# Retention layer: the product of scores and decay mask in two instructions, and a weighted sum that waits for each of them

## The reference

```
decay = log(1 - 2**(-5 - arange(H)))
mask = where(diff >= 0, exp(decay * diff), 0);  mask = mask / sqrt(mask.sum(-1))
qr = q * cos + rotate(q) * sin;   kr = k * cos + rotate(k) * sin
qk = einsum('bhsd,bhtd->bhst', qr, kr) * mask
qk = qk / clip(abs(qk.sum(-1)), 1)
out = einsum('bhst,bhtd->bhsd', qk, vr)
out = (out - mean) / sqrt(var + 1e-5);  out = silu(g) * out;  return out @ Wo + bo
```

## Time and profile before

| what | value |
|---|---|
| median of three runs | 3287.5 us (3285.61 to 3289.51) |
| span of the profiled execution, first to last instruction | 3276.3 us |
| PE busy | 2592.6 us, 79% of the span |
| DVE busy | 1690.3 us, 52% |
| ACT busy | 997.8 us, 30% |
| TensorE clock granted, mean | 0.915 of full |

### The profile page before, as it was taken

The page is one execution under the profiler, slowest core; times in us unless marked ns, Lnnn a source line. Parts: engine busy times, 40 slices in busy tenths (PEclk is TensorE's granted clock), DMA queues, the critical chain, the costliest instruction groups (busy, mean ns, idle before and its releaser), DMA issues.

```text
span 3276.3 us, 52997 instructions
## 1 busy us (share of the span) xinstructions
PE 2592.6 (79%) x23038; PEld 1853.6 (57%) x23038; DVE 1690.3 (52%) x4079; ACT 997.8 (30%) x1389; POOL 355.3 (11%) x605
## 2 busy tenths in 40 slices
PE   4666468888899887896778789777897778977778
PEld 2444156777777676664556455554555555555554
DVE  5666725656665654603376532665326654167540
ACT  3444312222232222031223432324323243232432
POOL 0111000111001100073010001100011000010000
PEclk8888559999999998898899999989999899998999
DMA  2000000000000000236400000000000000000000
GB/s 83 1 1 3 0 1 2 8 8 8 2 8 8 8 8 11 86 45 115 119 1 1 1 7 1 1 1 1 7 1 1 1 1 7 1 1 1 1 1 26
DMA packets 39354, 48.14 MB, mean 15 GB/s; under 512 B 7169, under 2 KB 36369, under 8 KB 38354
## 3 DMA queue, kind: packets, MB, share of 16 engines
q1 hardware_dynamic: 33490, 40.43, 4.2%
q0 software_dynamic: 5632, 4.33, 1.1%
HBM read 31.82 MB, written 12.91 MB: 14 GB/s over the span
## 4 chain that ended last, share of the span: by engine, by line
PE 56%; DVE 28%; ACT 7%; issue 4%; POOL 3%; DMA 1%; SPq 0%; DVEq 0%; POOLq 0%; ACTq 0%
PE banks L2397 7%; PE banks L871 6%; DVE wide_area L2273 4%; PE banks L2598 4%; DVE wide_area L1751 3%; PE banks L2386 2%; PE banks L1371 2%; PE banks L2171 2%; PE banks L1336 2%; PE banks L1170 2%; DVE xs L900 1%; PE banks L1404 1%; DVE weights L2090 1%; PE banks L1678 1%; PE banks L2180 1%
## 5 line engine op out<-in xcount | busy, mean ns | idle before, releaser
L2598 PE MATMUL banks<-wA 128*128 128x128 f32 x2664 | 362.8, 289 | 4.2 <-ACT xf L932 2.1
L2598 PEld LDWEIGHTS banks<-wA 128*128 128x128 f32 x2664 | 335.8, 202 | 23.2 <-issue 15.9
L892 DVE BATCH_NORM_STATS2 stats<-banks 128x6 f32<-128x128 f32 x208 | 46.4, 286 | 368.0 <-PE banks L871 340.4
L2273 DVE TENSOR_REDUCE wide_area<-banks 128x8 f32<-128x2048 f32 x64 | 146.8, 2293 | 106.8 <-PE banks L2171 106.8
L907 POOL TENSOR_TENSOR rstd<-moments,eps 128x4 f32<-128x4 f32 x56 | 11.2, 199 | 1454.9 <-DVE moments L896 1454.9
L2254 ACT ACTIVATE weights<-banks 128x2048 f32<-128x2048 f32 x64 | 120.1, 1877 | 99.5 <-PE banks L2180 99.5
L1751 DVE TENSOR_REDUCE wide_area<-banks 128x16 f32<-128x1024 f32 x80 | 94.1, 1218 | 43.9 <-PE banks L1664 43.5
L1717 ACT ACTIVATE weights<-banks 128x2048 f32<-128x2048 f32 x32 | 59.6, 1876 | 95.8 <-PE banks L1678 95.8
L2397 PE MATMUL banks<-wide_area,big 128*128 128x512 f32 x192 | 85.7, 592 | 0.0
L2090 DVE TENSOR_TENSOR weights<-banks,wC 128x2048 f32<-128x2048 f32 x32 | 72.2, 2287 | 24.1 <-PE banks L1977 24.1
L907 POOL TENSOR_TENSOR smalls<-smalls,eps 128x4 f32<-128x4 f32 x16 | 3.2, 199 | 726.2 <-DVE smalls L896 726.2
(11 more groups left out here) (765 smaller groups left out, 6077.1 us busy)
## 6 DMA issues: line engine op xcount, KB each, us to landing
big<-in_wE SPq DMA_DIRECT2D x1, 4096.0 KB, 13.9
weights<-long_kernel SPq DMA_DIRECT2D x8, 512.0 KB, 7.5
conv<-wide_area SPq DMA_DIRECT2D x16, 256.0 KB, 2.5
wC<-in_wC SPq DMA_DIRECT2D x1, 3012.0 KB, 17.3
wC<-in_wG SPq DMA_DIRECT2D x1, 2971.0 KB, 20.1
big<-in_wT SPq DMA_DIRECT2D x1, 2560.0 KB, 11.4
x_all<-in_xT SPq DMA_DIRECT2D x1, 2048.0 KB, 10.5
total<-spread SPq DMA_DIRECT2D x8, 256.0 KB, 2.3
```

What stands on the lines that cost most here:

```text
L892: dve.bn_stats(m.stats[:, i, :], self.tokens(i)).then_inc(*sg.up("dve", f"stats{i}"))
L2273: return dve.tensor_reduce(m.peaks[:, k % 2, :, :].rearrange("p t (r c) -> p r t c", r=4)[:, :, :, SPARE[j]], m.bank[:, :, :].rearrange("p ...
L2598: pe.matmul(bank[:, 0:P], m.ident, m.ident, start=True, stop=True)
```

## The change

The product becomes two instructions of 128 x 1024: `upper{i}` covers banks 0 and 1 (heads 0 to 7), `masked{i}` banks 2 and 3. Both follow the one wait for the scores. On PE the state group and the weighted sum are split in the same way: wait for `upper`, state matmuls and eight weighted sums of banks 0 and 1, then wait for `masked`, state matmuls and eight weighted sums of banks 2 and 3. The number of matmuls is the same. ACT still waits for the last of them.

```diff
-            dve += f" masked{i}{before} neg{i} denom{i} eps{i} sum{i} centre{i}{after}"
+            dve += f" upper{i} masked{i}{before} neg{i} denom{i} eps{i} sum{i} centre{i}{after}"
...
-            pe.wait_ge(*sg.done("dve", f"masked{i}", n))
-            if i % 2:
-                for r in range(4):
-                    rows = slice(32 * r, 32 * r + 32)
-                    pe.matmul(bank[:, r, 0:P], m.state[rows, i // 2, :], m.qf[rows, i * P:(i + 1) * P], start=True, stop=False)
-            for r in range(4):
-                for j in range(4):
-                    v = (i * H + 4 * r + j) * (HV + 1)
-                    mm = pe.matmul(bank[32 * j:32 * j + 32, r, 0:P], m.retflat[:, v:v + 32],
-                                   m.weights[:, (4 * r + j) * P:(4 * r + j + 1) * P], start=(i % 2 == 0), stop=True)
+            for step, half in (("upper", (0, 1)), ("masked", (2, 3))):
+                pe.wait_ge(*sg.done("dve", f"{step}{i}", n))
+                if i % 2:
+                    for r in half:
+                        rows = slice(32 * r, 32 * r + 32)
+                        pe.matmul(bank[:, r, 0:P], m.state[rows, i // 2, :], m.qf[rows, i * P:(i + 1) * P], start=True, stop=False)
+                for r in half:
+                    for j in range(4):
+                        v = (i * H + 4 * r + j) * (HV + 1)
+                        mm = pe.matmul(bank[32 * j:32 * j + 32, r, 0:P], m.retflat[:, v:v + 32],
+                                       m.weights[:, (4 * r + j) * P:(4 * r + j + 1) * P], start=(i % 2 == 0), stop=True)
...
-            dve.tensor_tensor(m.weights.rearrange("p (h q) -> p h q", h=H),
-                              bank[:, :, :].rearrange("p r (j q) -> p (r j) q", j=4),
-                              m.causal[:, 0:P].unsqueeze(1).broadcast_to([P, H, P]), ALU.mult).then_inc(*sg.up("dve", f"masked{i}"))
+            for step, half in (("upper", 0), ("masked", 1)):
+                dve.tensor_tensor(m.weights[:, half * 1024:half * 1024 + 1024].rearrange("p (h q) -> p h q", h=H // 2),
+                                  bank[:, 2 * half:2 * half + 2, :].rearrange("p r (j q) -> p (r j) q", j=4),
+                                  m.causal[:, 0:P].unsqueeze(1).broadcast_to([P, H // 2, P]), ALU.mult).then_inc(*sg.up("dve", f"{step}{i}"))
```

## The result

Beside the kernel before on the same chip the changed kernel took 3267.64 us (median of 6 runs, 3258.01 to 3273.84) against 3286.93 (6 runs, 3282.02 to 3290.99). The ratio of this comparison is 0.9925, 95% interval 0.9901 to 0.9949. It is not the quotient of these two medians, which is 0.9941 (19.3 us). The forecast, 3274.5 of 3287.5, is 0.9960. So the direction and the mechanism held. By its ratio the first comparison came out 12 us lower than forecast (0.9925 x 3287.5 = 3262.8, under the range's low end of 3267), by its medians 6 us lower (3268.2). The stage itself, read from the traces, gained 16 to 18 us where 13.0 were forecast.

A forecast was written before the change was run, and what follows sets the result against it. It took PE standing still for each pair's whole first product, much of it at 1.2 GHz, as the bound. Terms summed to 13.0 us: 3276.3 less 13.0 is 3263.3, plus 11.2 around the span 3274.5; range 3267 to 3289.

The forecast's parts named there:

- the mechanism: In the tile pairs, PE starts sums on the first half product; shorter gaps bring back the full clock: 13.0 us.
- the range's low end: Whole kernel: 3267 us, a little under 3268.7, the case with all of C's scores and free state groups (4.0 us more).
- A: First tile pair of an iteration: full clock before its second sum, gain 1.16 us in three iterations, 0.36 in one; 3.8.
- D: Last tile of lane 1, standing alone: no wait removed, second state group costs 0.43 us in each of four iterations; -1.7.
- B: Second tile pair of an iteration: PE's gap shortened and full clock kept, gain 1.06 us four times; 4.2.
- C: Third tile pair of an iteration: full clock back at about 1725.7, gain 1.3 us four times; 5.2.
- Rival 1: In the stage's tile pairs, the clock stays as it was and gains and losses cancel: 3287.5 us, chance 0.29.
- rival 2: Odd tiles: second state group and way back cost another 0.74 us (0.43 at full clock); 10.6 us slower, 3298, chance 0.11.
- The 12 waits of the earlier trace: PE's state groups waiting for the product: 11.5 us, read as one wait of some 1 us per pair, three pairs, four iterations.
- first tile: First tile of lane 0: its last half product comes later, uncovered, costing 0.08 us each, 0.3 us in all.
- C's scores: First scores of the third pair: 2.09 us to 1.17 at the full clock, counted in two iterations of four; 1.8.
- free state groups: Second state groups costing nothing: 0.43 us more in each A and D, some 0.15 in C; part of the 3268.7 case.

The follow-up runs named there:

- experiment 10: Kernel before, products whole, with scores of each pair's second tile repeated and 3, 5, 8 and 8 filler matmuls before later scores: 3259.04 us, ratio 0.9913.
- third trace: The changed kernel, unedited, compared a third time with the kernel before: 3271.83 us against 3285.68, ratio 0.9964.
- again: The changed kernel, unedited, timed and profiled a second time beside the kernel before: 3273.54 us against 3291.39, ratio 0.996.
- Experiment 9: The change in the three tile pairs only, plus 3, 5, 8 and 8 filler matmuls before scores (half an earlier run's count): 3261.6 us, ratio 0.9927.
- products only: The change with its product in two instructions, but PE waiting for both, sums and state groups whole: 3290.9 us, ratio 0.9977 to the kernel before.
- experiment 2: Kernel before, product whole, with scores of each pair's second tile computed over again while PE waits: 3271.56 us, ratio 0.9948.
- pairs only: The change without its split in lane 0's first and lane 1's last tile; second run, beside half the fillers: 3262.43 us, ratio 0.9931 to the kernel before.

## Why the prediction was right, and where it was not

**Right: the mechanism.** Split at the same full clock, the pairs gain 0.32, 0.31 and 0.30 us (A 5.99 to 5.67, B 5.55 to 5.24, C 5.55 to 5.25). That is 0.9 an iteration (44.31 to 43.33 from experiment 10 to 9; both have the same fillers, and the scores that 10 repeats fall into PE's waits), less 0.53 for D (0.45 on PE, the rest ahead of its state group): 0.4, some 1.6 us in the whole kernel. At the half clock C gained 0.2 (6.66 to 6.47) where nothing was forecast. So the sum for a clock that stays was near, and the rest of the 16 to 18 us is the clock, as forecast. Rival 1 fell with A and B off its intervals in all twelve iterations of the change's three traces, and with C off in ten. So did rival 2: the second state group costs what the forecast took, 0.43 forecast and 0.42 to 0.45 measured. The Trainium skill, TensorEngine Tiling (Array Packing), Key Properties, says that a switch of the tiling mode drains TensorE; no run here shows a state group without its switch, so that price isn't seen by itself and lies within the 0.45.

**Right: the pairs' own intervals.** A 5.63 forecast (1698.88 to 1704.51), 5.67 measured; B 5.20 (1709.59 to 1714.79), 5.24 measured. In the forecast it is DVE's last half that lets PE finish A, and the traces bear this out. A takes 5.67 us with its first 3 us at the half clock (the change, iteration 2) and at the full one (third trace, iteration 1):

```profile
2119.50:2122.50 3.00, 3.00 (x36) 1.13 (x32) 2.98 (x3) 0.00 (x0) 0.00 (x0) 0.50 0.02 5
```

```profile
1705.70:1708.70 3.00, 2.03 (x40) 0.77 (x35) 2.95 (x3) 0.00 (x0) 0.00 (x0) 1.00 0.00 0
```

**Misread, without moving the sum.** The 12 waits of the earlier trace rows are not one for each pair: they are the first waits of B and C and the second one of A, whose first stands on line 1988. That a pair's first wait is about 1 us comes out all the same. And the clock's fall at 1712.1 had more than a single gap before it:

```profile
1707.81 1.14 PE L1977 MATMUL banks<-spread,gates 32*128 32x512 f32 x8 [0.68 <-DVE segvals L2107]
```

**Mis-sized: what the clock gives around C and D.** The forecast's terms beside the gains that the three traces of the change show, in us over four iterations:

| stretch | forecast | change | again | third |
|---|---|---|---|---|
| first tile to A | -0.3 | -1.3 | -1.2 | 0.2 |
| A to B (term A) | 3.8 | 4.1 | 4.1 | 4.0 |
| B to C (B 4.2, C's scores 1.8) | 6.0 | 6.0 | 6.2 | 7.5 |
| C to D (term C) | 5.2 | 7.7 | 9.1 | 7.1 |
| D to its back transposes | -1.7 | -0.6 | -0.7 | -0.9 |
| sum | 13.0 | 16.0 | 17.5 | 17.9 |

The step that failed is C's. It counted the pair up to its transposes and stopped there, and C to D gave 7.1 to 9.1 us where it had 5.2. In the first trace C itself gave 4.4 (26.6 to 22.2 us, summed over four iterations) where 5.2 was counted; the transposes, `centre` and D's scores behind it gave the other 3.3 of C to D, at the full clock too, and had no term. Nor had D: it was partly at the half clock before (8.89 to 8.94 against 8.54 at the full one), so the clock paid back 0.4 of the 0.53 that its split costs. The reason given for counting C's scores in two iterations of four, that PE's gap of 2.60 us stays, held by luck in B to C (two of four in the first trace) and was wrong for D. The cost put on the first tile, 0.08 each, isn't seen (12.85 to A in the change's iteration 2, 12.86 before); what that stretch lost in two traces is the clock, which fell in it.

**The range's low end** took in C's scores and free state groups, and asked nowhere what the stage takes with no half clock at all. Experiment 9 shows that: 23.4 us less to D and 1.6 behind it (35.7 to 34.2), 25.0 in all. Less the 2.1 of D's split in the change that is 22.9, so some 3264.6 was the lowest that this stage could give. The stage's own 16.0 to 17.9 would have stayed in the range (3287.5 - 17.9 = 3269.6); the 24.7 us of the ratio 0.9925 are more than even the 22.9. Its interval, 16.8 to 32.5 us, includes the stage's 17.5 and 17.9.

**What stays open** is where the rest of those 24.7 us lies. By medians the three comparisons give 19.3, 17.9 and 13.9 us, around the stage's 16.0 to 17.9; by ratios they give 24.7, 13.2 and 11.8. The traces show parts that the change doesn't touch moving by as much (us: up to the first product; the four stages, each from the first tile's product to D's back transposes; the rest, between and behind them):

| profiled execution | ahead | stages | rest | span |
|---|---|---|---|---|
| before | 1685.9 | 232.4 | 1358.0 | 3276.3 |
| products only | 1699.2 | 233.2 | 1357.4 | 3289.8 |
| the change | 1691.7 | 216.4 | 1354.4 | 3262.6 |
| the change again | 1700.8 | 215.0 | 1357.7 | 3273.5 |
| the change, third | 1692.9 | 214.5 | 1351.1 | 3258.6 |

Before and products only have the same stage within 0.8 us, and yet 13.3 us lie between their starts of it. The change's second and third trace are 14.9 us apart, and 0.5 of that is in the stage. Such scatter can carry some us into a median of 6; I have no run that shows it did. The prediction also put 11.2 us around the span; in the changed kernel's profiled run it is 1.8 (3264.38 to 3262.6). Most of the 11.2 was the span of a short execution set beside a median, and it cancels in the sum only because 13.0 was taken from the median.

## What to carry to other kernels

Where a stage runs partly at 1.2 GHz, price a change twice, at the clock that stands and with the stage wholly at the full clock: here the first gave about nothing and the second 23 to 25 us, and the truth lay between. Compare such small changes by the stage in the traces as well: parts of this program that no edit touched moved by 13 us between two executions. An engine's wait for a product says little by itself: the fastest kernel here waits three times as long as the change, and does throwaway matmuls in between. Fit such matmuls to the gap by the trace's own duration for them, since what overruns is lost at once, and leave steps unsplit where no wait is removed.

## What the runs showed of the hardware that was not expected

- No single gap decides on the clock. In experiment 10 gaps of 0.82, 1.33 and 0.68 us follow one another in pair C and it stays at 1.00; the change kept it in iteration 2 behind a gap of 2.60; in the kernel before, it stood at half with gaps of 2.60 and 0.71. Filling PE's waits in the pairs alone, and leaving the 2.60, took the half clock from 105.8 to 27.3 us (experiment 2). The Trainium skill, TensorE: Matmul & The Clock Gate, section Why this matters for your kernels, lays a fallen clock to idle gaps longer than any of these; here shorter ones mattered, and the measurement decides.
- From pair B on, the same instructions at the same spacing lost the clock in one iteration and kept it in the next (C's scores and C, 0.52 and 1.00). What decides wasn't settled.
- A filler, a matmul with 128 fp32 columns, leaves two records and takes 0.23 to 0.24 us at the full clock (3.74 for 16, 1.95 for 8).
- Whether times scatter less with the clock held in the stage isn't shown. Whole products and fillers stayed within 3256.82 to 3263.13 in six runs, against 3260.37 to 3286.32 in the change's twelve beside them; but half the fillers, with no half clock in its stage either, spread over 3260.15 to 3270.38, and pairs only beside it over 3259.7 to 3268.97.
